# Norming of the heads before attention: query bias on TensorE, a square and a copy a tile, guard and scale in one step, three products on GpSimd

## The chip, the cores and the metric

One NeuronCore of one Trainium2 chip runs the whole program. Its engines are TensorE (PE; its weight loads are listed as PEld), VectorE (DVE), ScalarE (ACT), GpSimd (POOL) and SyncE (SP), which issues the transfers. Each engine works through its own list of instructions in the written order, and semaphores tie the lists together. The metric is the device time of one execution in microseconds; less is better.

## The reference, cut to what matters

Four sequences of 512 tokens with 256 channels pass through a bidirectional state-space block with a gated MLP and then through an attention block. The change lies in the attention block, between its layer norm and its scores:

```python
x1 = _ln(x) * (scale1 + 1.0) + shift1
qkv_bias = jnp.concatenate([q_bias, jnp.zeros_like(q_bias), v_bias])
qkv = (x1 @ mat_qkv_w.T + qkv_bias).reshape(B, L, 3, H, hd)
q, k, v = [jnp.transpose(qkv[:, :, i], (0, 2, 1, 3)) for i in range(3)]
sm = jnp.exp(jnp.minimum(scale_mul, MAX_SCALE_MUL))
q = _l2norm(q) * sm          # x / max(sqrt(sum(x * x)), 1e-12), H = 16 heads of hd = 16
k = _l2norm(k)
scores = jnp.einsum('bhqd,bhkd->bhqk', q, k)
```

So each of 16 query heads and 16 key heads of a token is divided by its length, and the query heads are scaled by a factor of their own. Only queries and values have a bias. All data are in fp32.

## The kernel before, in words

The program goes through the four sequences one after another (`batch(b)`). In each it scans 128 rows of the state-space block (the greater part of the time), then comes the residual, the MLP, the attention and the feed-forward part. The order on each engine is written out by hand; nothing is scheduled by a planner. Tokens are worked in `TT` = 4 tiles of 128. PSUM has 8 banks of 128x512 fp32, named `bank0` to `bank7`; all of them are handed from one use to the next by semaphores.

The stage that changes runs like this. The residual after the MLP is added tile by tile by VectorE (`residual_ln`, L1540), which also makes the statistics and `x_norm` (L1531). TensorE turns each tile's `x_norm` (`ln_turn`, L983) into banks 6 and 7, ScalarE shifts and scales it into `h_t` (L757), and TensorE multiplies `h_t` by the query and key weights (L1286), 128x512 a tile, into banks 4 and 5 in turn. VectorE adds the query bias on the way out (L1716, the semaphore `q_ready`), ScalarE copies the key half (L898) and squares both halves in two steps (L899, L900, `sq_ready`), VectorE sums the squares by head (L1694), ScalarE takes the root (L894), and VectorE guards it (L1699), inverts it (L1701), multiplies by the scales `qk_scale` (L1703) and multiplies the heads by the result (`unit`, L1706) into `qk_pad`, where each head has 32 lanes. Meanwhile TensorE makes the values (`value_tile`): a product of one row of ones (`ident[0:1, 0:1]` spread out) with the bias row (L1296) and two with the weights (L1299). Then it turns the normed heads (`turn_heads`, L1313) into banks 6 and 7; VectorE and ScalarE copy them to `q_t` and `k_t` (L1726, L913), and the scores begin (L1348), whose least values VectorE takes (`least`, L1732). GpSimd has nothing to do from its clearing of `qk_pad` on until `qk_unit` tells that all four products are done; then it weights the projection and later weights with the gates (L718 and on).

Buffers are reused, and the profile names them by their first owner: `inflow_tok` holds `qk`, `h_t` and the MLP's product `ab`; `states` holds `qk_sq`; `b_diag` holds the sums and their inverses; `decay` holds `qk_pad`; `dt` and `dtx_tok` hold `q_t` and `k_t`; `silu_z` holds the values. An fp32 product is recorded as two matmul records, a transpose as one; the order of the program counts products and transposes once each.

Of the kernel before, what the change touches and what calls it, by code (L numbers as in the profile page):

```python
# [7 lines left out]
ALU = mybir.AluOpType  # L8
ACT = mybir.ActivationFunctionType
# [64 lines left out]
QK_BANK = 4  # L74
# [67 lines left out]
def build(nc, inp, out):  # L142
    ctx = ExitStack()
    with ctx:
# [35 lines left out]
        qk_scale = sb("qk_scale", [P, 2 * H])  # L180
# [64 lines left out]
        norm_max = norm_sq  # L245
# [44 lines left out]
        q_scale_ready = sem("q_scale_ready")  # L290
# [82 lines left out]
        q_ready = sem("q_ready")  # L373
        k_ready = sem("k_ready")
# [4 lines left out]
        norm_max_ready = sem("norm_max_ready")  # L379
        norm_inv_ready = sem("norm_inv_ready")  # L380
        qk_inv_ready = sem("qk_inv_ready")
        qk_unit = sem("qk_unit")
        qk_turned = sem("qk_turned")
# [37 lines left out]
        out_rows = out.rearrange("b (t p) d -> b p t d", p=P)  # L421

# [189 lines left out]
        def _(pool):  # L612
# [5 lines left out]
            pool.memset(qk_scale[:, H:2 * H], -1.0).then_inc(sign_ready, 1)  # L618
# [69 lines left out]
            def batch(b, last):  # L688
# [26 lines left out]

                pool.wait_ge(res_ready, (b * 2 + 1) * TT)
                pool.wait_ge(qk_unit, (b + 1) * TT)
# [25 lines left out]
        def _(act):  # L743
# [4 lines left out]

            def ln(b, i):
# [20 lines left out]
                if i == 2:  # L770
                    for t in range(TT):
                        root(t)
                        if t:
                            shift(t - 1)
                    shift(TT - 1)
                    return
                root(0)
                root(1)
                shift(0)
                shift(1)  # L780
# [73 lines left out]
            for s in range(NS):  # L854
                if s == DT_EXP_AT[0]:
                    act.wait_ge(ssm_loaded, 16 * len(SSM))
                    act.activation(a_exp[:], a_log[:], ACT.Exp).then_inc(a_exp_done, 1)
                    act.wait_ge(cap_ready, 1)
                    act.wait_ge(sign_ready, 1)
                    act.activation(qk_scale[:, 0:H], scale_cap[:], ACT.Exp).then_inc(q_scale_ready, 1)  # L860
# [4 lines left out]
            def batch(b, last):  # L865
# [26 lines left out]
                def root(t):  # L892
# [3 lines left out]
                for t in range(TT):  # L896
                    act.wait_ge(q_ready, b * TT + t + 1)
                    act.activation(qk[:, t, D:2 * D], banks[QK_BANK + t % 2][:, D:2 * D], ACT.Copy)  # L898
                    act.activation(qk_sq[:, t, D:2 * D], banks[QK_BANK + t % 2][:, D:2 * D], ACT.Square).then_inc(k_ready, 1)  # L899
                    act.activation(qk_sq[:, t, 0:D], qk[:, t, 0:D], ACT.Square).then_inc(sq_ready, 1)  # L900
                    if t:
                        root(t - 1)
                root(TT - 1)
# [45 lines left out]
        def _(pe):  # L949
# [270 lines left out]
            def batch(b, last):  # L1220
# [49 lines left out]
                for t in range(TT):  # L1270
# [7 lines left out]
                    last.then_inc(res_mm, 1)  # L1278
                ln_turn(b, 2, 1)
                for t in range(TT):  # L1280
                    ln_wait(b, 2, t)
                    pe.wait_ge(res_ready, (b * 2 + 1) * TT + t + 1)
                    if t > 1:
                        pe.wait_ge(k_ready, b * TT + t - 1)
                    for kc in range(KD):
                        last = pe.matmul(banks[QK_BANK + t % 2], h_t[:, kc, t * P:(t + 1) * P], qkv_w[:, kc, 0:2 * D],  # L1286
                                         start=(kc == 0), stop=(kc == KD - 1))
                    last.then_inc(qk_mm, 1)
                    if t == 0:
                        ln_turn(b, 2, 2)  # L1290
                        ln_turn(b, 2, 3)

                def value_tile(t):

                    to = banks[V_BANK + t // 2][:, t % 2 * D:(t % 2 + 1) * D]
                    pe.matmul(to, ident[0:1, 0:1].to_broadcast([1, P]), row_b[0:1, V_BIAS, :], start=True, stop=False,  # L1296
# [536 lines left out]
```

## Time and profile before

| what | us |
|---|---|
| median of 3 runs | 3185.71 (3183.74 to 3186.26) |
| the profiled execution | 3181.57 |
| its span, first to last instruction | 3179.80 |
| TensorE busy in the span | 3101.2 (98%) |
| VectorE busy | 2759.0 (87%) |
| ScalarE busy | 2705.0 (85%) |
| GpSimd busy | 2484.5 (78%) |

All times below are microseconds from the start of the span. A row of a timeline merges neighbouring instructions of one kind: its second number runs from the start of the first to the end of the last, and the end of a matmul is modelled, so that the start of the next row is the surer mark. "idle before" in brackets tells how long the engine had stood idle and what ended it. The stage occurs four times, with its first head turn at about 740.6, 1520.6, 2301.6 and 3063.6.

### The profile page before, as it was taken

The numbers are of one execution on the slowest core, as the hardware profiler recorded it, in microseconds if no ns is written. First come the engines' busy times: TensorE is split into PE (matmuls) and PEld (weight loads), VectorE is DVE, ScalarE is ACT, GpSimd is POOL, SyncE is SP. The second block draws the span as 40 slices with busy tenths as digits, with TensorE's granted clock in tenths as the row PEclk, the third lists the DMA queues.
The fourth block names the chain that finished last, engine by engine and source line by source line (L and its number), as shares of the span: only waits on it lengthen the run. The fifth ranks groups of instructions, "written<-read, shape, count | busy, mean of one in ns | idle before, by whom it ended". The sixth has DMA issues, their size and how long they took to land.

```text
span 3179.8 us, 59519 instructions
## 1 busy us (share of the span) xinstructions
PE 3101.2 (98%) x23304; PEld 2630.3 (83%) x23304; DVE 2759.0 (87%) x3049; ACT 2705.0 (85%) x4496; POOL 2484.5 (78%) x638
## 2 busy tenths in 40 slices
PE   7999999999999999999999999999999999999999
PEld 6998899884699889988479988998748998888955
DVE  3999999977399999997659999999666999999963
ACT  4999999965699999995579999999458999999845
POOL 2999999971299999995139999999415999999910
PEclk9999999999999999999999999999999999999999
DMA  5222222210222222221022222222102222222100
GB/s 188 77 82 67 90 69 82 74 56 29 75 67 82 80 86 67 89 86 58 1 83 70 89 82 78 79 77 88 45 14 80 81 80 85 74 70 82 57 14 8
DMA packets 195239, 225.69 MB, mean 71 GB/s; under 512 B 77448, under 2 KB 149640, under 8 KB 193680
## 3 DMA queue, kind: packets, MB, share of 16 engines
q1 hardware_dynamic: 194960, 221.89, 22.7%
q8 instruction: 185, 3.03, 0.4%
q14 instruction: 94, 0.77, 0.1%
HBM read 217.37 MB, written 4.48 MB: 70 GB/s over the span
## 4 chain that ended last, share of the span: by engine, by line
PE 78%; POOL 11%; issue 5%; DVE 3%; ACT 1%; DMA 1%; SPq 0%; DVEq 0%; ACTq 0%; POOLq 0%
PE bank L1124 21%; PE bank L1104 16%; PE bank L1004 10%; PE bank L1105 9%; POOL states L669 7%; PE bank L1348 4%; PE bank L1100 4%; POOL y_gated L669 4%; PE bank L1369 2%; PE bank L1381 2%; PE bank L1483 2%; DVE states L1630 1%; PE bank L1179 1%; PE bank L1131 1%; PE bank L1276 1%
## 5 line engine op out<-in xcount | busy, mean ns | idle before, releaser
L669 POOL TENSOR_TENSOR states<-states,c_rows 128x2048 f32<-128x2048 f32 x336 | 1532.8, 4582 | 129.1 <-DVE states L1630 126.8
L1630 DVE TENSOR_TENSOR_SCAN states<-decay,bank 128x512 f32<-128x512 f32 x1376 | 1577.1, 1200 | 16.5 <-ACT decay L849 1.2
L849 ACT ACTIVATE decay<-dt,a_log 128x512 f32<-128x512 f32 x2048 | 1305.5, 710 | 0.0
L840 ACT ACTIVATE inflow_tok<-dtx_tok,b_tok 128x512 f32<-128x512 f32 x1536 | 995.6, 713 | 81.0 <-PE bank L1105 70.4
L1104 PE MATMUL bank<-ident,inflow_tok 128*128 128x128 f32 x5280 | 903.4, 280 | 35.6 <-DVE states L1630 18.4
L1124 PE MATMUL bank<-ident,states 128*128 128x128 f32 x5504 | 825.5, 273 | 6.1 <-DVE y_gated L1636 3.0
L1630 DVE TENSOR_TENSOR_SCAN y_gated<-decay,bank 128x512 f32<-128x512 f32 x672 | 776.7, 1201 | 12.3 <-issue 2.6
L669 POOL TENSOR_TENSOR y_gated<-y_gated,c_rows 128x2048 f32<-128x2048 f32 x168 | 770.0, 4583 | 17.8 <-DVE y_gated L1630 16.1
L1104 PEld LDWEIGHTS bank<-ident,inflow_tok 128*128 128x128 f32 x5280 | 597.7, 140 | 205.7 <-issue 88.0
L1105 PE MATMUL bank<-b_diag,dtx_tok 128*128 128x128 f32 x3520 | 680.5, 275 | 0.0
L1124 PEld LDWEIGHTS bank<-ident,states 128*128 128x128 f32 x5504 | 644.6, 141 | 14.2 <-POOL states L669 7.7
L1105 PEld LDWEIGHTS bank<-b_diag,dtx_tok 128*128 128x128 f32 x3520 | 531.5, 191 | 0.0
L1124 PE MATMUL bank<-ident,y_gated 128*128 128x128 f32 x2688 | 403.5, 273 | 1.3 <-POOL y_gated L669 0.7
L1124 PEld LDWEIGHTS bank<-ident,y_gated 128*128 128x128 f32 x2688 | 315.0, 141 | 4.6 <-POOL y_gated L669 3.8
L735 POOL TENSOR_TENSOR part<-part,x_in 128x1024 f32<-128x1024 f32 x4 | 9.4, 2354 | 302.0 <-ACT part L767 302.0
L1732 DVE TENSOR_REDUCE decay<-bank 128x1 f32<-128x512 f32 x256 | 158.9, 682 | 45.3 <-PE bank L1348 45.2
L1004 PE MATMUL bank<-xs,xproj_w 128*128 128x256 f32 x640 | 185.2, 381 | 0.9 <-ACT b_tok L812 0.5
L1348 PE MATMUL bank<-dtx_tok,dt 32*128 32x512 f32 x512 | 155.4, 693 | 3.1 <-ACT dtx_tok L913 3.1
L1100 PE MATMUL bank<-ident,inflow_tok 128*128 128x128 f32 x864 | 149.1, 282 | 0.9 <-DVE states L1630 0.5
L927 ACT ACTIVATE y_gated<-bank 128x512 f32<-128x512 f32 x176 | 92.7, 601 | 59.6 <-PE bank L1369 59.1
L718 POOL TENSOR_TENSOR x_in<-proj_w,gate 128x512 f32<-128x512 f32 x4 | 5.1, 1272 | 165.9 <-DVE decay L1706 165.9
L1100 PEld LDWEIGHTS bank<-ident,inflow_tok 128*128 128x128 f32 x864 | 97.6, 140 | 33.5 <-DVE states L1630 6.4
(174 smaller groups left out, 2596.6 us busy)
## 6 DMA issues: line engine op xcount, KB each, us to landing
c_rows<-c_spill SPq DMA_DIRECT2D x256, 512.0 KB, 3.7
b_diag<-diag_ring SPq DMA_DIRECT2D x256, 128.0 KB, 2.3
xproj_w<-in_xproj_w SPq DMA_DIRECT2D x32, 320.0 KB, 3.7
in_w<-in_in_w SPq DMA_DIRECT2D x16, 512.0 KB, 4.6
out_w<-in_out_w SPq DMA_DIRECT2D x4, 1024.0 KB, 8.2
in_w<-in_fc_w SPq DMA_DIRECT2D x8, 512.0 KB, 4.1
xproj_w<-in_w SPq DMA_DIRECT2D x8, 512.0 KB, 5.2
xproj_w<-in_fc_w SPq DMA_DIRECT2D x4, 1024.0 KB, 4.8
```

Of the source, the lines that this page charges most:

```text
L669: pool.tensor_tensor(state_row, state_row, c_row.to_broadcast([P, KI, L]), ALU.mult).then_inc(weighed, PAIRS)
L840: last_tok = act.activation(inflow_tok[:, r % SLOTS, t, :], dtx_tok[:, d, t, :], ACT.Copy, scale=b_tok[:, d, t, s:s + 1])
L849: act.activation(decay[:, r % SLOTS * KI + k, :], dt[:, d, k, :], ACT.Exp, scale=a_neg[:, d, k, s:s + 1]).then_inc(decay_ready, 1)
L927: act.activation(probs_t[v % len(probs_t)], banks[t_bank(v)], ACT.Exp, scale=-1.0).then_inc(probs_t_ready, 1)
L1004: out = pe.matmul(to[:, c], lhs, rhs[:, c], start=start and half == 0, stop=stop, skip_group_check=True)
L1100: last = pe.transpose(to[:, t * P:(t + 1) * P], tile[:, k * P:(k + 1) * P], ident[:])
L1104: pe.transpose(to[:, t * P:(t + 1) * P], inflow_tok[:, r % SLOTS, t, k * P:(k + 1) * P], ident[:])
L1105: pe.matmul(to[:, (TT - 1) * P:TT * P], dtx_tok[:, d, TT - 1, k * P:(k + 1) * P], b_diag[:, r % DIAGS, :], start=True, stop=True).then_inc ...
L1124: last = pe.matmul(banks[KI + t][:, k * P:(k + 1) * P], state_slots[r % STATES][:, k, t * P:(t + 1) * P], ident[:], is_transpose=True, sta ...
L1348: pe.matmul(score_bank(u), q_t[a, g, t * P:(t + 1) * P], k_t[a, g, :], start=True, stop=True).then_inc(scores_mm, 1)
L1630: dve.tensor_tensor_scan(state_slots[r % STATES][:, k, time], decay[:, slot, time], banks[k % INFLOW_BANKS][:, time], 0.0, ALU.mult, ALU.a ...
L1732: dve.tensor_reduce(qk_pad[:, t, g, lane:lane + 1], score_bank(u), AX.X, ALU.min).then_inc(neg_ready, 1)
```

## The change

The query bias is no longer added by VectorE: TensorE puts it into the bank with a one-row product (`query_bias`) ahead of the query and key products, which then add to it. The four tiles get banks 4, 5, 0 and 1, one each, and no longer wait for `k_ready`; and the turns of tiles 1 to 3 stand at other places. ScalarE squares a whole tile of 512 columns from the bank in one step and copies it in another; the first square stands among the shifts of `ln`. VectorE guards the root and multiplies by the inverse scale in one step (`inv_scale`, made at the start by an exponential of the negated exponent), then inverts. The products of tiles 0 to 2 are made by GpSimd from ScalarE's copy, that of tile 3 by VectorE straight from the bank, so tile 3 needs no copy.

```diff
-QK_BANK = 4
+QK_BANKS = (4, 5, 0, 1)
...
+                for t in range(TT - 1):
+                    pool.wait_ge(qk_copied, b * (TT - 1) + t + 1)
+                    pool.wait_ge(norm_inv_ready, b * TT + t + 1)
+                    pool.tensor_tensor(heads(qk_pad[:, t, :, :].rearrange("p g c -> p (g c)"), LANE)[:, :, 0:HD],
+                                       heads(qk[:, t, :], HD), norm_inv[:, t, :].unsqueeze(2).to_broadcast([P, 2 * H, HD]),
+                                       ALU.mult).then_inc(qk_unit, 1)
+
                 pool.wait_ge(res_ready, (b * 2 + 1) * TT)
-                pool.wait_ge(qk_unit, (b + 1) * TT)
                 pool.tensor_tensor(proj_g, proj_w[:], gate[:, GAMMA1, :].unsqueeze(1).to_broadcast([P, KD, D]),
                                    ALU.mult).then_inc(proj_gated, 1)
...
+            def square(b, t):
+
+                act.wait_ge(qk_mm, b * TT + t + 1)
+                act.activation(qk_sq[:, t, :], banks[QK_BANKS[t]], ACT.Square).then_inc(sq_ready, 1)
+
...
-                if i == 2:
-                    for t in range(TT):
-                        root(t)
-                        if t:
-                            shift(t - 1)
-                    shift(TT - 1)
-                    return
+                if i == 2:
+                    root(2)
+                    shift(1)
+                    root(3)
+                    shift(2)
+                    square(b, 0)
+                    shift(3)
+                    return
...
-                    act.activation(qk_scale[:, 0:H], scale_cap[:], ACT.Exp).then_inc(q_scale_ready, 1)
+                    act.activation(inv_scale[:, 0:H], scale_cap[:], ACT.Exp, scale=-1.0).then_inc(inv_scale_ready, 1)
...
-                def root(t):
+                def head_root(t):
-                for t in range(TT):
-                    act.wait_ge(q_ready, b * TT + t + 1)
-                    act.activation(qk[:, t, D:2 * D], banks[QK_BANK + t % 2][:, D:2 * D], ACT.Copy)
-                    act.activation(qk_sq[:, t, D:2 * D], banks[QK_BANK + t % 2][:, D:2 * D], ACT.Square).then_inc(k_ready, 1)
-                    act.activation(qk_sq[:, t, 0:D], qk[:, t, 0:D], ACT.Square).then_inc(sq_ready, 1)
-                    if t:
-                        root(t - 1)
-                root(TT - 1)
+                def copy_heads(t):
+                    act.activation(qk[:, t, :], banks[QK_BANKS[t]], ACT.Copy).then_inc(qk_copied, 1)
+                copy_heads(0)
+                square(b, 1)
+                head_root(0)
+                copy_heads(1)
+                square(b, 2)
+                head_root(1)
+                square(b, 3)
+                copy_heads(2)
+                head_root(2)
+                head_root(3)
...
+                def query_bias(t):
+                    pe.wait_ge(res_ready, (b * 2 + 1) * TT + t - 1)
+                    pe.matmul(banks[QK_BANKS[t]][:, 0:D], ident[0:1, 0:1].to_broadcast([1, P]), row_b[0:1, Q_BIAS, :], start=True,
+                              stop=False, skip_group_check=True)
+                def heads_tile(t):
+                    ln_wait(b, 2, t)
+                    for kc in range(KD):
+                        last = pe.matmul(banks[QK_BANKS[t]], h_t[:, kc, t * P:(t + 1) * P], qkv_w[:, kc, 0:2 * D],
+                                         start=False, stop=(kc == KD - 1), skip_group_check=True)
+                    last.then_inc(qk_mm, 1)
+                query_bias(0)
+                query_bias(1)
-                for t in range(TT):
-                    ln_wait(b, 2, t)
-                    pe.wait_ge(res_ready, (b * 2 + 1) * TT + t + 1)
-                    if t > 1:
-                        pe.wait_ge(k_ready, b * TT + t - 1)
-                    for kc in range(KD):
-                        last = pe.matmul(banks[QK_BANK + t % 2], h_t[:, kc, t * P:(t + 1) * P], qkv_w[:, kc, 0:2 * D],
-                                         start=(kc == 0), stop=(kc == KD - 1))
-                    last.then_inc(qk_mm, 1)
-                    if t == 0:
-                        ln_turn(b, 2, 2)
-                        ln_turn(b, 2, 3)
+                query_bias(2)
+                heads_tile(0)
+                ln_turn(b, 2, 2)
+                query_bias(3)
+                heads_tile(1)
+                ln_turn(b, 2, 3)
+                heads_tile(2)
+                heads_tile(3)
+                    pe.wait_ge(res_ready, (b * 2 + 1) * TT + V_BANK + t // 2 + 1)
...
-                            pe.wait_ge(qk_unit, b * TT + t + 1)
+                            if t < TT - 1:
+                                pe.wait_ge(qk_unit, b * (TT - 1) + t + 1)
+                            else:
+                                pe.wait_ge(qk_unit_last, b + 1)
...
-                def unit(t):
+                def invert(t):
-                    dve.tensor_scalar(norm_max[:, t, :], norm[:, t, :], EPS_NORM, None, ALU.max).then_inc(norm_max_ready, 1)
-                    dve.wait_ge(norm_max_ready, b * TT + t + 1)
-                    dve.reciprocal(norm_inv[:, t, :], norm_max[:, t, :]).then_inc(norm_inv_ready, 1)
-                    dve.wait_ge(norm_inv_ready, b * TT + t + 1)
-                    dve.tensor_tensor(norm_inv[:, t, :], norm_inv[:, t, :], qk_scale[:], ALU.mult).then_inc(qk_inv_ready, 1)
-                    dve.wait_ge(qk_inv_ready, b * TT + t + 1)
-                    pad = qk_pad[:, t, :, :].rearrange("p g (h e) -> p (g h) e", e=LANE)
-                    dve.tensor_tensor(pad[:, :, 0:HD], qk[:, t, :].rearrange("p (h e) -> p h e", e=HD),
-                                      norm_inv[:, t, :].unsqueeze(2).to_broadcast([P, 2 * H, HD]),
-                                      ALU.mult).then_inc(qk_unit, 1)
+                    dve.scalar_tensor_tensor(norm_over[:, t, :], norm[:, t, :], EPS_NORM, inv_scale[:], ALU.max,
+                                             ALU.mult).then_inc(norm_over_ready, 1)
+                    dve.wait_ge(norm_over_ready, b * TT + t + 1)
+                    dve.reciprocal(norm_inv[:, t, :], norm_over[:, t, :]).then_inc(norm_inv_ready, 1)
-                    dve.wait_ge(q_scale_ready, 1)
+                    dve.wait_ge(inv_scale_ready, 1)
-                for t in range(TT):
-                    dve.wait_ge(qk_mm, b * TT + t + 1)
-                    dve.tensor_tensor(qk[:, t, 0:D], banks[QK_BANK + t % 2][:, 0:D], row_b[:, Q_BIAS, :],
-                                      ALU.add).then_inc(q_ready, 1)
-                    if t:
-                        sum_squares(t - 1)
-                    if t > 1:
-                        unit(t - 2)
-                sum_squares(TT - 1)
-                unit(TT - 2)
-                unit(TT - 1)
+                sum_squares(0)
+                sum_squares(1)
+                invert(0)
+                sum_squares(2)
+                invert(1)
+                sum_squares(3)
+                invert(2)
+                invert(3)
+                dve.wait_ge(norm_inv_ready, (b + 1) * TT)
+                dve.tensor_tensor(heads(qk_pad[:, TT - 1, :, :].rearrange("p g c -> p (g c)"), LANE)[:, :, 0:HD],
+                                  heads(banks[QK_BANKS[TT - 1]], HD), norm_inv[:, TT - 1, :].unsqueeze(2).to_broadcast([P, 2 * H, HD]),
+                                  ALU.mult).then_inc(qk_unit_last, 1)
```

On TensorE, from the product with `w3` (into bank 3) to the first value tile, there stood before:

```order
L1276 MATMUL bank3<-w3,inflow_tok 128x256 x4
L983 MATMUL bank7<-ident,x_norm 128x128 [waits ln_norm]
L1286 MATMUL bank4<-qkv_w,inflow_tok 128x512 [waits res_ready,ln_ready]
L983 MATMUL bank6<-ident,x_norm 128x128 [waits ln_ready,ln_norm]
...
L983 MATMUL bank7<-ident,x_norm 128x128 [waits ln_ready,ln_norm]
...
L1286 MATMUL bank5<-qkv_w,inflow_tok 128x512 [waits res_ready,ln_ready]
...
L1286 MATMUL bank5<-qkv_w,inflow_tok 128x512 [waits k_ready,res_ready,ln_ready]
...
L1296 MATMUL bank2<-row_b,ident 128x256
```

In the changed kernel (L1296 is there the product with `w3`, L1302 the query bias, L1003 the turn, L1309 the heads' product, L1329 the value bias) the same stretch of TensorE reads:

```order
L1296 MATMUL bank3<-w3,inflow_tok 128x256 x4
L1302 MATMUL bank4<-row_b,ident 128x256 [waits res_ready]
L1302 MATMUL bank5<-row_b,ident 128x256 [waits res_ready]
L1003 MATMUL bank7<-ident,x_norm 128x128 [waits ln_norm]
...
L1302 MATMUL bank0<-row_b,ident 128x256 [waits res_ready]
L1309 MATMUL bank4<-qkv_w,inflow_tok 128x512 [waits ln_ready]
...
L1003 MATMUL bank6<-ident,x_norm 128x128 [waits ln_ready,ln_norm]
...
L1302 MATMUL bank1<-row_b,ident 128x256 [waits res_ready]
L1309 MATMUL bank5<-qkv_w,inflow_tok 128x512 [waits ln_ready]
...
L1003 MATMUL bank7<-ident,x_norm 128x128 [waits ln_ready,ln_norm]
...
L1329 MATMUL bank2<-row_b,ident 128x256 [waits res_ready]
```

Four one-row products are new. The turn of tile 1 now stands behind two of them, and the turn of tile 3 has moved from ahead of the heads of tile 1 to behind them.

On VectorE the norming of the last tile, from its sum of squares (tile 2's steps behind it are left out) to the first copy of the turned heads, was this before:

```order
L1694 TENSOR_REDUCE b_diag<-states 128x32 [waits sq_ready]
...
L1699 TENSOR_SCALAR b_diag<-b_diag 128x32 [waits norm_ready]
L1701 RECIPROCAL b_diag<-b_diag 128x32 [waits norm_max_ready]
L1703 TENSOR_TENSOR b_diag<-b_diag,qk_scale 128x32 [waits norm_inv_ready]
L1706 TENSOR_TENSOR decay<-inflow_tok,b_diag 128x32x16 [waits qk_inv_ready]
L1726 COPY dt<-bank6 128x512 [waits qk_turned]
```

The changed kernel has at the same place of VectorE's list:

```order
L1730 TENSOR_REDUCE b_diag<-states 128x32 [waits sq_ready]
...
L1735 SCALAR_TENSOR_TENSOR b_diag<-b_diag,inv_scale 128x32 [waits norm_ready]
L1738 RECIPROCAL b_diag<-b_diag 128x32 [waits norm_over_ready]
L1753 TENSOR_TENSOR decay<-bank1,b_diag 128x32x16 [waits norm_inv_ready]
L1757 COPY dt<-bank6 128x512 [waits qk_turned]
```

Two steps of three remain between root and product, and one product of four; the other three stand on GpSimd's list between the clearing of `silu_z` and the weighting of the projection:

```order
L717 MEMSET silu_z 128x2048
L722 TENSOR_TENSOR decay<-inflow_tok,b_diag 128x32x16 [waits norm_inv_ready,qk_copied] x3
L727 TENSOR_TENSOR x_in<-proj_w,gate 128x512 [waits res_ready]
L729 TENSOR_TENSOR x_in<-row_b,gate 128x256
L730 TENSOR_TENSOR x_in<-row_b,gate 128x256
```

GpSimd no longer waits for `qk_unit` ahead of the weighting; it does the three products itself, each after a tile's inverse and copy.

## Rows read from the trace of the kernel before

**Rows 1.** The page's chain that ended last, by engine.

```profile
PE 78%; POOL 11%; issue 5%; DVE 3%; ACT 1%; DMA 1%; SPq 0%; DVEq 0%; ACTq 0%; POOLq 0%
```

**Rows 2.** Chain in order of time, first batch: start us, us, what.

```profile
727.84 0.50 DVE x_norm L1531
...
728.38 0.44 PE bank L983 x2
...
740.76 0.89 PE bank L1313 x8
...
741.67 0.61 ACT dtx_tok L913
```

**Rows 3.** Timeline of TensorE, first batch: start us, us, instructions, idle before.

```profile
723.70 1.89 PE L1276 MATMUL bank<-w,inflow_tok 128*128 128x256 f32 x8
725.43 0.38 PE L983 MATMUL bank<-ident,x_norm 128*128 128x128 f32 x2
725.64 1.88 PE L1286 MATMUL bank<-qkv_w,inflow_tok 128*128 128x512 f32 x4
727.36 0.38 PE L983 MATMUL bank<-ident,x_norm 128*128 128x128 f32 x2
728.38 0.44 PE L983 MATMUL bank<-ident,x_norm 128*128 128x128 f32 x2 [0.63 <-DVE x_norm L1531]
728.65 5.37 PE L1286 MATMUL bank<-qkv_w,inflow_tok 128*128 128x512 f32 x12
733.95 0.69 PE L1296 MATMUL bank<-row_b,ident 1*128 1x256 f32 x2
734.58 1.13 PE L1299 MATMUL bank<-qkv_w,inflow_tok 128*128 128x256 f32 x4
735.64 0.69 PE L1296 MATMUL bank<-row_b,ident 1*128 1x256 f32 x2
...
740.60 1.04 PE L1313 MATMUL bank<-ident,decay 128*128 128x128 f32 x8
```

**Rows 4.** Timeline, all engines, first batch.

```profile
739.90 0.69 DVE L1706 TENSOR_TENSOR decay<-inflow_tok,b_diag 128x512 f32<-128x512 f32 x1
...
740.38 1.01 PEld L1313 LDWEIGHTS bank<-ident,decay 128*128 128x128 f32 x8
```

**Rows 5.** Timeline of TensorE, second batch.

```profile
1508.42 0.44 PE L983 MATMUL bank<-ident,x_norm 128*128 128x128 f32 x2 [0.63 <-DVE x_norm L1531]
...
1520.64 1.04 PE L1313 MATMUL bank<-ident,decay 128*128 128x128 f32 x8
```

**Rows 6.** Groups of instructions: xcount | busy us, mean ns | idle before.

```profile
L913 ACT ACTIVATE dtx_tok<-bank 128x512 f32<-128x512 f32 x16 | 9.5, 593 | 1.1 <-PE bank L1313 1.1
L1694 DVE TENSOR_REDUCE b_diag<-states 128x32 f32<-128x512 f32 x16 | 10.8, 676 | 0.0
L894 ACT ACTIVATE b_diag<-b_diag 128x32 f32<-128x32 f32 x16 | 3.7, 229 | 6.1 <-DVE b_diag L1694 6.1
L1701 DVE RECIPROCAL b_diag<-b_diag 128x32 f32<-128x32 f32 x16 | 5.6, 353 | 0.5
L1706 DVE TENSOR_TENSOR decay<-inflow_tok,b_diag 128x512 f32<-128x512 f32 x16 | 11.1, 691 | 0.5
L718 POOL TENSOR_TENSOR x_in<-proj_w,gate 128x512 f32<-128x512 f32 x4 | 5.1, 1272 | 165.9 <-DVE decay L1706 165.9
```

**Rows 7.** Windows: us, PE, PEld, DVE, ACT, POOL busy, clock, DMA.

```profile
754.00:758.00 4.00, 4.00 (x15) 1.89 (x16) 4.00 (x8) 0.83 (x2) 0.62 (x1) 0.69 0.02 4
1534.00:1538.00 4.00, 4.00 (x15) 1.86 (x12) 4.00 (x8) 0.05 (x1) 0.68 (x1) 0.50 0.00 0
```

**Rows 8.** Timeline, scores of first and second batch.

```profile
756.00 1.11 PE L1355 MATMUL bank<-ident,decay 128*128 128x128 f32 x4
...
1536.80 1.11 PE L1355 MATMUL bank<-ident,decay 128*128 128x128 f32 x4
```

**Rows 9.** Line L1680: duration ns min/median/max, first and last start.

```profile
L1680 DVE TENSOR_TENSOR states<-states,c_rows x8: 678/1594/3253, 686.6 to 3012.6; 128x512 f32<-128x512 f32 x8
```

More of the change, by code:

```diff
@@ L179, in build @@
         scale_cap = sb("scale_cap", [P, H])
-        qk_scale = sb("qk_scale", [P, 2 * H])
+        inv_scale = sb("inv_scale", [P, 2 * H])
         proj_w = sb("proj_w", [P, KD, D])
@@ L244, in build @@
         norm = norm_sq
-        norm_max = norm_sq
+        norm_over = norm_sq
         norm_inv = b_diag[:, HALF + 1, :].rearrange("p (t h) -> p t h", t=TT)
@@ L289, in build @@
         cap_ready = sem("cap_ready")
-        q_scale_ready = sem("q_scale_ready")
+        inv_scale_ready = sem("inv_scale_ready")
         mod_mm = sem("mod_mm")
@@ L372, in build @@
         v_mm = sem("v_mm")
-        q_ready = sem("q_ready")
-        k_ready = sem("k_ready")
+        qk_copied = sem("qk_copied")
         v_ready = sem("v_ready")
@@ L378, in build @@
         norm_ready = sem("norm_ready")
-        norm_max_ready = sem("norm_max_ready")
+        norm_over_ready = sem("norm_over_ready")
         norm_inv_ready = sem("norm_inv_ready")
-        qk_inv_ready = sem("qk_inv_ready")
         qk_unit = sem("qk_unit")
+        qk_unit_last = sem("qk_unit_last")
         qk_turned = sem("qk_turned")
@@ L421, in build, with heads @@
         out_rows = out.rearrange("b (t p) d -> b p t d", p=P)
+        def heads(row, e):
+            return row.rearrange("p (h e) -> p h e", e=e)
         def lead_last(bank):
@@ L617, in _ @@
             pool.memset(ring_zeros, 0.0).then_inc(zeros_ready, 1)
-            pool.memset(qk_scale[:, H:2 * H], -1.0).then_inc(sign_ready, 1)
+            pool.memset(inv_scale[:, H:2 * H], -1.0).then_inc(sign_ready, 1)
             pool.memset(minus_half[:], -0.5).then_inc(half_ready, 1)
```

## The prediction

> **What bounds the kernel now.** I read the page's chain first: TensorE carries 78% of the path that ended last and VectorE 3% [rows 1]. That average covers several stages, so I followed the chain in time through the one that changes, the norming of the heads in the first batch [rows 2]. The reader is to see who holds the path there. Until 728.33 it is VectorE with the last `x_norm`; from 728.38 to 741.65 it is TensorE alone: a turn (L983), the query and key products of three tiles (L1286), the four value tiles (L1296 and L1299), the turn of the normed heads (L1313). Only then does ScalarE take over with `dtx_tok`, the copy of the turned keys. VectorE's adds, sums and products do not appear.
>
> Then the timeline of TensorE [rows 3]. Its rows follow one another without a gap except once: the turn of tile 2 starts at 727.36 and that of tile 3 at 728.38, 1.02 us later, where a turn and its neighbour are otherwise 0.21 us apart (725.43 to 725.64). So 0.81 us are spent waiting for `x_norm`, and nothing else is. VectorE is close behind, however: its last product runs from 739.90 to 740.59, while the weights of the first turn are loaded at 740.38 and the turn starts at 740.60 [rows 3, 4]. Tile 3 is the fourth of those transposes, so the product is out before it is needed, by a few tenths. The second batch has the same gap of 0.63 us ahead of the turn and 12.22 us from it to the first head turn (1508.42 to 1520.64), as the first has (728.38 to 740.60) [rows 3, 5]. Thus two chains end almost together, and a gain on VectorE's alone is worth nothing until TensorE's becomes shorter.
>
> **The change part by part.** *TensorE gets four bias products a batch.* An operation of this shape stands in the trace: the value bias L1296, one row by 256 columns. A value tile, from one bias to the next, takes 735.64 - 733.95 = 1.69 us for six records of 256 columns. Eight such records without a bias, in tile 3 of the product with `w3`, take 725.43 - 723.70 = 1.73 us, 0.216 us each [rows 3]. Six would take 1.30, so 0.39 us of each value tile is lost around its bias. A bias that stands alone between full products therefore costs 2 x 0.216 + 0.39 = 0.82 us; the pair of tiles 0 and 1, which stand together, 4 x 0.216 + 0.39 = 1.25. Both ends: nothing lost (0.43 each, 1.73 for four) or the loss paid by each of the four (3.28). I take 0.82 twice and 1.25 once, 2.89 us, since the row is of the same operands and sizes. The Trainium skill says, in TensorEngine Tiling (Array Packing), section Key Properties, that changing the tiling mode drains TensorE. By that rule each run of one-row products pays at entry and exit, which agrees with the 0.39 us; without it the four would cost only their columns. The rule speaks against this change.
>
> *TensorE loses its wait.* The turn of tile 3 now stands behind the products of tile 1, long after its `x_norm`, so the 0.81 us go. Written out from the old rows, in the first batch: the product with `w3` ends at 725.43, the pair of biases at 726.68, turn 1 at 726.89, the bias of tile 2 at 727.71, the heads of tile 0 (1.72 us, 725.64 to 727.36) at 729.43, turn 2 at 729.64, the bias of tile 3 at 730.46, heads 1 at 732.18, turn 3 at 732.39, heads 2 at 734.11, heads 3 at 735.83. The old values and turn took 740.60 - 733.95 = 6.65 after 0.14 us of change-over, so the first head turn starts at about 742.62 in place of 740.60: 2.02 us later in a batch. The waits that the bias products carry (`res_ready` of the attention's input) are for residuals of tiles finished before them; the value tiles' waits likewise. `k_ready` is no longer waited for, but the rows show no gap in the twelve products, so this gives nothing. Each heads tile needs its `h_t`; ScalarE makes it under 1 us after a turn, in the same order as before, and every turn now precedes its heads by over a microsecond.
>
> *The norming chain gets shorter, under cover of TensorE.* VectorE loses four adds, four guards and three products, gains none. ScalarE's copy of 512 columns out of a bank costs 593 ns by L913, and I take the same for a square of 512; a sum of squares 676, a root 229, a reciprocal 353, the one-step guard and scale about what a small two-input step takes, estimated at 0.2; the last product 691 [rows 6]. After heads 2 (734.11, landed 0.2 later) there remain at most two squares, one copy, three roots, two sums, three guards with reciprocals and the product: 1.78 + 0.69 + 1.35 + 1.66 + 0.69 = 6.2 us if nothing overlapped, so 740.5 at the latest. GpSimd's products have the size of L718, 1272 ns. The first reciprocal follows turn 3 (732.39) by a shift, a copy, a square and a root on ScalarE and a guard on VectorE, at an estimated 736.2, and three products end at 740.0 if not held up. All of this lies before 742.62; the cover is 2.1 us, and a delay beyond it would be paid in full.
>
> *Behind the turn* nothing is rearranged. GpSimd's gated weights start after its last product, near where they started (740.74). ScalarE's value and key copies and VectorE's first copy follow TensorE as they did, and the scores after them, so the 2.02 us move the rest of the batch whole. Four batches: 8.1 us. The profiled execution took 3181.57 us, 1.77 more than its span, and lies 4.1 below the median of the runs, 3185.71, and under the fastest of them. The same step on its time gives 3189.7, on the median 3193.8.
>
> *The clock.* In the scores that follow, the granted clock falls to its lower level: 0.69 as a mean over 754 to 758 in the first batch, 0.50 (1.2 GHz) over 1534 to 1538 in the second [rows 7]. TensorE was just then running the 32-row score products, waiting for VectorE between them. The turn L1355 then starts 15.40 us after the first head turn in the first batch (740.60 to 756.00), 16.16 in the second (1520.64 to 1536.80) [rows 3, 5, 8]. A shifted stage can meet that fall earlier or later: 0.76 us a batch, from -2.3 us (three batches become like the first) to +0.8.
>
> **The rivals.** *The bias products hide (3182.5).* If each cost under 0.2 us, the 0.81 us removed would outweigh them; were they free, the turns would start 0.81 us earlier, VectorE's chain being then out in time, and the result is 3185.7 - 3.2 = 3182.5, no change that can be measured. It would need gaps in TensorE's rows, and there is one of 0.81 us, while two records cannot stream in less than 0.43. For it: only that record ends are modelled. Chance 0.09.
>
> *Only the columns count (3189.1).* If the 0.39 us belong to the value tiles and not to a bias, the three losses go: 2.02 - 1.17 = 0.85 a batch, 3.4 in all. Against it: L1296 starts and L1299 starts are 0.63 apart, again and again. Chance 0.14.
>
> *VectorE and GpSimd get in each other's way (3203).* L1680, a VectorE step with two operands in SBUF, took 678 to 3253 ns for 512 columns, beside GpSimd's last weighing; L1706 with the same shape and GpSimd idle took 691 [rows 6, 9]. In the changed kernel each guard step reads two SBUF tiles while GpSimd multiplies the tile before. If each of the guards of tiles 1 to 3 waited out a product, the products would start at 736.2, 738.1 and 739.9, and VectorE's own would end at about 742.5: just hidden. It decides from there: if reciprocals or sums waited too, two more products, 2.5 us, would reach the path, 745.0, and the total is 4.4 us a batch, 3185.7 + 17.6 = 3203. The Trainium skill, GPSIMD Engine Reference, section Key points, names this contention for two-SBUF-input steps; the range of L1680 agrees, and by that rule alone the guards would wait and the products not. Chance 0.08.
>
> **How the numbers follow.** The forecast has 0.69. Its own range is 3191.5 to 3196.2: from the clock's -2.3 to the loss paid by all four biases (+1.6) with the clock's +0.8. For 8 in 10 I reach down past the columns-only case, 3187.5, and up to 3198. A measurement of this kernel can tell about 0.2%, 6.4 us, from no change: slower means over 3192.1. The forecast lies above that unless clock and spread (the runs before range over 2.5 us) take 1.7 us from it; I give it 0.62 of its 0.69. With the collision, slower 0.70; the other part and the two rivals that end lower make 0.30, of which 0.04 goes to faster, for biases that hide and a clock that falls kindly in all batches, and 0.26 to the same.
>
> **What would show it.** Right: bias rows on TensorE 0.63 us ahead of what follows, no idle before the turn of tile 3, the path through the stage TensorE throughout, the first head turn some 2.0 us later after the end of the product with `w3` (17.2 us against 15.2), VectorE's last product over early. Wrong: head turns that wait for GpSimd or VectorE; bias products at 0.43 us; or a start of the turns before 17 us.

## The result

The changed kernel takes 3191.86 us (median of 9 runs, 3187.87 to 3198.38), the kernel before 3183.28 in the same comparison (9 runs, 3181.40 to 3186.26): ratio 1.0028, interval 1.0019 to 1.0037, so some 6 to 12 us slower. The profiled execution took 3191.34 us, with a span of 3189.6, 9.8 more than before.

In the chain that ended last, TensorE has gained four points [rows 1]:

```profile
PE 82%; POOL 8%; issue 4%; DVE 3%; ACT 2%; DMA 1%; SPq 0%; DVEq 0%; ACTq 0%; POOLq 0%
```

The timeline of TensorE in the first batch, as [rows 3] before (L1296 is the product with `w3`, L1302 the query bias, L1003 a turn, L1309 the heads, L1329 and L1332 the values, L1349 the head turns):

```profile
723.09 1.89 PE L1296 MATMUL bank<-w,inflow_tok 128*128 128x256 f32 x8
724.91 1.13 PE L1302 MATMUL bank<-row_b,ident 1*128 1x256 f32 x4
725.97 0.44 PE L1003 MATMUL bank<-ident,x_norm 128*128 128x128 f32 x2
726.34 0.69 PE L1302 MATMUL bank<-row_b,ident 1*128 1x256 f32 x2
726.96 1.98 PE L1309 MATMUL bank<-qkv_w,inflow_tok 128*128 128x512 f32 x4
728.78 0.38 PE L1003 MATMUL bank<-ident,x_norm 128*128 128x128 f32 x2
729.09 0.69 PE L1302 MATMUL bank<-row_b,ident 1*128 1x256 f32 x2
729.72 1.98 PE L1309 MATMUL bank<-qkv_w,inflow_tok 128*128 128x512 f32 x4
731.54 0.38 PE L1003 MATMUL bank<-ident,x_norm 128*128 128x128 f32 x2
731.75 3.60 PE L1309 MATMUL bank<-qkv_w,inflow_tok 128*128 128x512 f32 x8
735.28 0.69 PE L1329 MATMUL bank<-row_b,ident 1*128 1x256 f32 x2
...
741.93 1.04 PE L1349 MATMUL bank<-ident,decay 128*128 128x128 f32 x8
```

No row carries an idle time any more. From the start of the last tile of the product with `w3` to the first head turn it is 741.93 - 723.09 = 18.84 us, where it was 740.60 - 723.70 = 16.90 [rows 3]: 1.94 us more. The four batches have 1.94, 1.95, 1.93 and 1.94, 7.8 us together. Each bias that stands alone starts 0.62 or 0.63 us ahead of its heads (726.34 to 726.96), the pair 1.06 ahead of the turn.

The timelines of VectorE and GpSimd in the same stretch show the norming (L1735 is the guard with the scale, L1738 the reciprocal, L722 GpSimd's product, L1753 VectorE's):

```profile
735.09 1.06 POOL L722 TENSOR_TENSOR decay<-inflow_tok,b_diag 128x512 f32<-128x512 f32 x1 [36.48 <-DVE b_diag L1738]
...
735.46 0.73 DVE L1735 SCALAR_TENSOR_TENSOR b_diag<-b_diag,inv_scale 128x32 f32<-128x32 f32 x1
...
736.72 1.06 POOL L722 TENSOR_TENSOR decay<-inflow_tok,b_diag 128x512 f32<-128x512 f32 x1 [0.58 <-DVE b_diag L1738]
...
737.04 0.79 DVE L1735 SCALAR_TENSOR_TENSOR b_diag<-b_diag,inv_scale 128x32 f32<-128x32 f32 x1
...
738.13 0.13 DVE L1735 SCALAR_TENSOR_TENSOR b_diag<-b_diag,inv_scale 128x32 f32<-128x32 f32 x1
...
738.65 1.06 POOL L722 TENSOR_TENSOR decay<-inflow_tok,b_diag 128x512 f32<-128x512 f32 x1 [0.87 <-DVE b_diag L1738]
738.68 0.69 DVE L1753 TENSOR_TENSOR decay<-bank,b_diag 128x512 f32<-128x512 f32 x1
```

All four products are out by 739.71, 2.2 us ahead of the turns. Two of the guards take 0.73 and 0.79 us where one without a neighbour takes 0.13, and they end when GpSimd's product does (735.46 + 0.73 = 736.19, against 735.09 + 1.06 = 736.15).

### The profile page after: what moved, and what is told of

The parts are those of the page before. It is cut to its first block, busy times and chain, and to the rows that moved or that the text cites. A ratio compares the mean times of both kernels' runs of the same rounds, so it can differ in the third digit from the quotient of the medians.

```text
span 3189.6 us, 59523 instructions
## 1 busy us (share of the span) xinstructions
PE 3111.6 (98%) x23336; PEld 2637.1 (83%) x23336; DVE 2745.7 (86%) x3005; ACT 2704.2 (85%) x4476; POOL 2496.2 (78%) x650
## 4 chain that ended last, share of the span: by engine, by line
PE 82%; POOL 8%; issue 4%; DVE 3%; ACT 2%; DMA 1%; SPq 0%; DVEq 0%; ACTq 0%; POOLq 0%
PE bank L1144 23%; PE bank L1124 17%; PE bank L1024 10%; PE bank L1125 10%; POOL states L672 5%; PE bank L1120 4%; PE bank L1384 4%; POOL y_gated L672 2%; PE bank L1405 2%; PE bank L1417 2%; PE bank L1519 2%; DVE states L1666 2%; PE bank L1199 1%; PE bank L1309 1%; PE bank L1151 1%
## 5 line engine op out<-in xcount | busy, mean ns | idle before, releaser
L1124 PEld LDWEIGHTS bank<-ident,inflow_tok 128*128 128x128 f32 x5280 | 597.5, 141 | 210.8 <-issue 93.4
L722 POOL TENSOR_TENSOR decay<-inflow_tok,b_diag 128x512 f32<-128x512 f32 x12 | 12.7, 1057 | 150.7 <-DVE b_diag L1738 150.7
L1405 PE MATMUL bank<-dt,dtx_tok 32*128 32x512 f32 x512 | 125.0, 630 | 0.0
```

Source lines behind the costliest of these rows:

```text
L1124: pe.transpose(to[:, t * P:(t + 1) * P], inflow_tok[:, r % SLOTS, t, k * P:(k + 1) * P], ident[:])
L1405: pe.matmul(banks[t_bank(v)], k_t[a, g, kt * P:(kt + 1) * P], q_t[a, g, :], start=True, stop=True).then_inc(scores_t_mm, 1)
```

## The experiments

Three rivals to the forecast's account were to be settled: only the columns cost; GpSimd and VectorE hold each other up; part of the loss lies elsewhere. The table sums up what the timelines gave, per batch, from the start of the product with `w3` to the first head turn ("the stage" below) and to the first score product. These are its marks in TensorE's timeline of the first batch, before and after, which with the head turns at 740.60 and 741.93 give the first two rows:

```profile
718.16 5.34 PE L1276 MATMUL bank<-w,inflow_tok 128*128 128x256 f32 x24
742.41 1.13 PE L1348 MATMUL bank<-dtx_tok,dt 32*128 32x512 f32 x4 [0.78 <-ACT dtx_tok L913]
```

```profile
717.55 5.34 PE L1296 MATMUL bank<-w,inflow_tok 128*128 128x256 f32 x24
743.74 1.13 PE L1384 MATMUL bank<-dtx_tok,dt 32*128 32x512 f32 x4 [0.78 <-ACT dtx_tok L933]
```

The ratios are to the kernel before as it ran beside each; its medians there were 3183.18 to 3184.10. A ratio whose interval holds 1 shows no change.

| kernel | head turn, us | first score, us | median, us | ratio (interval) |
|---|---|---|---|---|
| before | 22.44 | 24.25 | 3183.28 | 1 |
| after | 24.38 | 26.19 | 3191.86 | 1.0028 (1.0019 to 1.0037) |
| no query bias | 21.54 | 23.36 | 3179.51 | 0.9988 (0.9980 to 0.9997) |
| query bias, 128 rows | 23.26 | 25.08 | 3189.14 | 1.0018 (1.0009 to 1.0027) |
| both biases, 128 rows | 21.71 | 23.52 | 3180.02 | 0.9990 (0.9981 to 0.9999) |
| before, turn moved | 23.31 | 25.13 | 3186.89 | 1.0012 (1.0003 to 1.0021) |
| and own banks | 21.54 | 23.70 | 3180.72 | 0.9993 (0.9984 to 1.0002) |
| and values, 128 rows | 19.98 | 23.70 | 3192.84 | 1.0028 (1.0019 to 1.0038) |
| and TensorE kept busy | 19.98 | 23.71 | 3181.17 | 0.9994 (0.9985 to 1.0003) |
| after, products twice | 24.38 | 26.20 | 3195.55 | 1.0040 (1.0027 to 1.0053) |
| both 128 rows, value behind | 20.41 | 22.92 | 3180.99 | 0.9991 (0.9982 to 0.9999) |

**No query bias.** The four products are left out, and with them the query bias. The wait that they carried and the opening of the bank pass to the heads' product (not shown).

```diff
...
-                query_bias(0)
-                query_bias(1)
                 ln_turn(b, 2, 1)
-                query_bias(2)
                 heads_tile(0)
                 ln_turn(b, 2, 2)
-                query_bias(3)
                 heads_tile(1)
...
```

> The changed kernel with its four query-bias products left out (so the query bias is not added at all); everything else of the change stays. Theory (the four one-row products on TensorE are the whole loss, the rest lies under TensorE's cover): from the start of the product with w3 to the first head turn 24.38 - 2.75 = 21.6 us, 0.8 us a batch less than before the change, no idle on TensorE ahead of the turns; about 3.2 us faster than before, ratio 0.999. Rival (part of the loss comes from GpSimd's products, the guards or the squares): the stage stays above 22.4 us, with head turns that wait for GpSimd or VectorE, and the time is not below that of before.

In the first batch the product with `w3` and the head turns start here:

```profile
716.57 5.34 PE L1296 MATMUL bank<-w,inflow_tok 128*128 128x256 f32 x24
...
738.11 1.04 PE L1346 MATMUL bank<-ident,decay 128*128 128x128 f32 x8
```

That is 21.54 us, as in every batch, 2.84 less than with the products and 0.90 less than before; the rest of the change is then a small gain, 0.9988. The whole loss is the four products.

**Query bias by 128 rows.** The bias tile holds the same row in all 128 partitions, so the identity times it is the bias on every token.

```diff
-                    pe.matmul(banks[QK_BANKS[t]][:, 0:D], ident[0:1, 0:1].to_broadcast([1, P]), row_b[0:1, Q_BIAS, :], start=True,
+                    pe.matmul(banks[QK_BANKS[t]][:, 0:D], ident[:], row_b[:, Q_BIAS, :], start=True,
                               stop=False, skip_group_check=True)
```

> The changed kernel, but the query bias is put in by the identity and all 128 (equal) rows of the bias tile, so that these products have the same 128 rows as their neighbours. Theory (0.39 us are lost around each run of one-row products, three runs a batch): the stage becomes 24.38 - 1.17 = 23.2 us, ratio to before 1.0012, about 4.7 us below the changed kernel. Rival (only the columns cost, the loss belongs to something else): the stage stays at 24.4 us and the ratio at 1.0028.

23.26 us: 1.12 of the expected 1.17 come back, with the same columns streamed. The timeline of TensorE now has 0.44 from a bias to its heads where 0.62 stood; the columns-only rival falls. The ratio, 1.0018, has the expected 1.0012 within its interval.

```profile
724.11 1.89 PE L1296 MATMUL bank<-w,inflow_tok 128*128 128x256 f32 x8
...
726.70 0.38 PE L1003 MATMUL bank<-ident,x_norm 128*128 128x128 f32 x2
726.92 0.60 PE L1302 MATMUL bank<-row_b,ident 128*128 128x256 f32 x2
727.36 1.88 PE L1309 MATMUL bank<-qkv_w,inflow_tok 128*128 128x512 f32 x4
729.07 0.38 PE L1003 MATMUL bank<-ident,x_norm 128*128 128x128 f32 x2
```

The loss goes with the change between one row and 128, not with each product: up to turn 1, behind the pair of biases, 0.29 us come back (2.88 to 2.59), up to turn 2, behind a single one, 0.44 (2.81 to 2.37), and up to turn 3 another 0.39. The weight loads show what changed. These are the loads for the bias of tile 2 and for the heads of tile 0, in the changed kernel and, below, in this run:

```profile
726.33 0.29 PEld L1302 LDWEIGHTS bank<-row_b,ident 1*128 1x128 f32 x2 [0.17 <-issue]
726.96 0.30 PEld L1309 LDWEIGHTS bank<-qkv_w,inflow_tok 128*128 128x128 f32 x2 [0.33 <-ACT inflow_tok L771]
```

```profile
726.81 0.30 PEld L1302 LDWEIGHTS bank<-row_b,ident 128*128 128x128 f32 x2
727.14 0.41 PEld L1309 LDWEIGHTS bank<-qkv_w,inflow_tok 128*128 128x128 f32 x2
```

By 128 rows the heads' weights are loaded from 727.14 on, 0.22 us ahead of their product (727.36) and while the bias still runs; behind one row the load starts at 726.96, with the product. The loads of the bias take no longer by one row (0.29 against 0.30), so the spread-out element as weights, which this edit removes too, is not what costs. Why a change of rows keeps the load back, no run shows.

**Both biases by 128 rows.** The same edit in `value_tile` as well.

> As the run before, and the four value biases as well by the identity and 128 rows. Theory (the loss of 0.39 us is at every one-row product between full ones): another 4 x 0.39 = 1.56 us a batch, the stage 21.65 us, 0.8 us a batch less than before the change; ratio 0.999. Rival (only the columns cost): 24.4 us and 1.0028. If VectorE's or GpSimd's chain becomes the later one, TensorE shows an idle time ahead of the head turns and the stage ends between 21.65 and 22.4.

21.71 us, another 1.55 for the expected 1.56. Two value biases in TensorE's timeline of the first batch:

```profile
737.84 0.59 PE L1329 MATMUL bank<-row_b,ident 128*128 128x256 f32 x2
739.14 0.59 PE L1329 MATMUL bank<-row_b,ident 128*128 128x256 f32 x2
```

A value tile takes 739.14 - 737.84 = 1.30 us, the six records' worth that the prediction worked out; it was 1.69 [rows 3]. This version keeps the change and is faster than both kernels; than the one before by 0.1%, with an interval that ends just under 1 (0.9981 to 0.9999).

**The kernel before with the turn moved.**

```diff
-                    if t == 0:
-                        ln_turn(b, 2, 2)
-                        ln_turn(b, 2, 3)
+                    if t < 2:
+                        ln_turn(b, 2, t + 2)
```

> The kernel before with one edit: the turn of tile 3 stands behind the heads of tile 1, as in the changed kernel. Theory (TensorE is the path, the wait ahead of that turn costs 0.81 us, and VectorE's chain moves up with the earlier heads): the stage goes from 22.44 to 21.6 us, 3.2 us in all, ratio 0.999. Rival (VectorE's chain of adds, sums and products is the bound as soon as TensorE is earlier): the head turns wait for its last product, the stage stays between 22.0 and 22.4 us, ratio 1.000.

Neither: 23.31 us, 0.87 more than before. The chain in order of time shows why (L757 is ScalarE's shift of tile 3, L898 and L899 its copy and square of tile 0):

```profile
728.18 0.80 ACT inflow_tok L757 x2
728.98 0.27 ACT inflow_tok L898
729.26 0.28 ACT states L899
729.54 0.14 issue
729.67 3.67 PE bank L1286 x8
```

TensorE's timeline has the wait:

```profile
729.67 3.67 PE L1286 MATMUL bank<-qkv_w,inflow_tok 128*128 128x512 f32 x8 [1.53 <-ACT states L899]
```

The heads of tile 2 go into tile 0's bank and wait for `k_ready`, and ScalarE comes to tile 0 only behind the shift that the moved turn allows. Whether the moved turn pays with a bank for each tile is the next run's question.

**And own banks.** As the run before, with `QK_BANKS = (4, 5, 0, 1)` and without the wait for `k_ready`.

> The kernel before with two edits: the turn of tile 3 behind the heads of tile 1, and banks 4, 5, 0 and 1, one for each tile, so that no heads product waits for ScalarE's squares of an earlier tile. Theory (the 1.5 us that the moved turn cost by itself were the wait for the shared bank, k_ready): TensorE's own work needs 21.6 us from the product with w3 to the head turns, where 22.44 stood, and VectorE's chain, some 10 us from its first sum to its last product, now ends last, at an estimated 22.0: head turns at 21.6 to 22.0, ratio 0.9990 to 0.9995. Rival (the wait was not for the bank): the stage stays at 23.3 and the ratio at 1.0012.

TensorE is ready at 21.54 us, 1.77 earlier than with two banks and 0.90 earlier than before; the wait was for the bank. Its row of head turns is then stretched by VectorE, as the chain in order of time shows (L1703 is the norming's product, L1310 a turn):

```profile
739.76 0.70 DVE decay L1703
740.46 0.04 issue
740.50 0.78 PE bank L1310 x5
```

Tile 3's product ends at 740.46, 22.1 us after the start at 718.35, and the last five turns stand behind it. The first score comes at 23.70, 0.55 ahead of before; the ratio, 0.9993, is as forecast, but its interval holds 1.

**And value biases by 128 rows.**

> As the run before, with the value biases by the identity and 128 rows. Theory (two chains end together, and VectorE's longer norming bounds the stage once TensorE's is shorter): TensorE would be ready at 20.1 us but the last head turn of the first four waits for VectorE's product; the stage and the time are those of the run before to 0.3 us a batch. Rival (TensorE alone sets the stage): 20.1 us, 9 us faster than before, ratio 0.997.

The stage is as the theory had it: TensorE ready at 19.98, first score at 23.70 as in the run before. But the time is 9 us longer than before, and 12 longer than in the run before, which no theory here expected. The timeline of TensorE and the windows (us, busy of PE, PEld, DVE, ACT, POOL, granted clock, DMA) of the first batch:

```profile
738.05 0.38 PE L1310 MATMUL bank<-ident,decay 128*128 128x128 f32 x2
738.80 0.33 PE L1310 MATMUL bank<-ident,decay 128*128 128x128 f32 x1 [0.36 <-DVE decay L1703]
740.23 0.76 PE L1310 MATMUL bank<-ident,decay 128*128 128x128 f32 x5 [1.10 <-DVE decay L1703]
741.77 2.07 PE L1345 MATMUL bank<-dtx_tok,dt 32*128 32x512 f32 x4 [0.78 <-ACT dtx_tok L913]
```

```profile
741.00:743.00 2.00, 1.23 (x4) 0.53 (x4) 0.28 (x1) 0.60 (x1) 2.00 (x4) 0.57 0.02 4
743.00:749.00 6.00, 6.00 (x22) 3.39 (x21) 2.51 (x5) 1.36 (x3) 6.00 (x2) 0.50 0.00 0
```

TensorE stands idle for 0.36, 1.10 and 0.78 us, and between 741 and 743 the granted clock falls to its lower level, 1.2 GHz (0.57 as the mean of this window, 0.50 from 743 on): the first four score records take 2.07 us where they took 1.13. The first batch went so, and the fourth; there the first turn of the greatest values came 42.7 and 41.2 us after the start, in the two others, with the same waits, 38.1 and 37.7. What decides between them is not shown.

**And TensorE kept busy.** Four identity products without use fill the two waits for VectorE.

```diff
+                            if not g and not i:
+                                for _ in range((0, 0, 1, 3)[t]):
+                                    pe.matmul(banks[TURN_BANK + 1][:, 0:D], ident[:], qkv_w[:, 0, 0:D], start=True, stop=True)
                             pe.wait_ge(qk_unit, b * TT + t + 1)
```

> The run with own banks and value biases by 128 rows (ratio 1.0028, though its first scores came as early as in the run with own banks alone, 23.7 us after the start of the product with w3), plus four identity products of 256 columns (0.43 us each, result unused) that TensorE makes while it waits for VectorE: one ahead of the third head turn, three ahead of the fourth. Theory (the wait itself costs nothing more than with own banks alone; the loss came from the granted clock, which fell to its lower level right behind that wait in two of four batches and made the first scores twice as slow): with TensorE occupied the clock stays at its upper level until the scores, the first turn of the greatest values comes 37.2 to 38.1 us after the start in every batch, ratio 0.999 to 1.000. Rival (the loss has another cause, such as the order of the copies): the fillers change nothing or add up to 0.2 us a batch, ratio 1.003.

The first score at 23.71 as before, the clock at 1.00 in the windows where it had been 0.57 and 0.50, the greatest values' turn at 37.1 to 38.1 in all four batches, ratio 0.9994; so the clock was the loss:

```profile
741.00:743.00 2.00, 1.23 (x6) 0.50 (x7) 0.39 (x2) 0.60 (x1) 2.00 (x4) 1.00 0.01 4
743.00:749.00 6.00, 6.00 (x45) 3.52 (x45) 4.96 (x8) 3.26 (x6) 6.00 (x2) 1.00 0.00 0
```

This is also the fair measure for the rest of the change. With the value biases by 128 rows in both, the old norming and the bias on VectorE, given own banks and a busy TensorE, have the first score at 23.71; the new norming, shared with GpSimd, with the query bias on TensorE by 128 rows, has it at 23.52. That is 0.19 us a batch, and the ratios, 0.9994 and 0.9990, cannot be told apart.

**Products twice.** Each of GpSimd's three products is made twice in the changed kernel, with a wait for the first between.

> The changed kernel with each of GpSimd's three products made twice, with a wait for the first between. Theory (GpSimd's products and the guards that wait beside them end 2.2 us ahead of the head turns that read them, and this cover is all that hides them): 3 x 1.06 = 3.2 us more and a tenth for each wait, so 1.0 to 1.5 us a batch come to the path, the head turn of tile 2 waits for GpSimd, ratio 1.004 to 1.005. Rival (GpSimd's work is far from the path): no change, ratio 1.0028. Other rival (guards wait out each product in full and pass it on): 3 us or more a batch, ratio above 1.006.

A miss in size: the head turns stay at 24.38 and the first score at 26.20, so nothing reaches the path. Timelines of the first batch:

```profile
735.51 1.06 POOL L723 TENSOR_TENSOR decay<-inflow_tok,b_diag 128x512 f32<-128x512 f32 x1 [36.49 <-DVE b_diag L1743]
...
740.95 1.06 POOL L727 TENSOR_TENSOR decay<-inflow_tok,b_diag 128x512 f32<-128x512 f32 x1
...
742.35 1.04 PE L1354 MATMUL bank<-ident,decay 128*128 128x128 f32 x8
```

The sixth product ends at 742.01, 0.34 ahead of the turns. I had added 3.2 us to the old end, but the products had stood 0.6 and 0.9 us apart, waiting for inverses, and the extra ones filled these gaps. The ratio, 1.0040 from four runs, lies in the forecast range, but not for its reason: the stage does not show it, and the interval overlaps with that of 1.0028.

**A value tile behind the head turns.** From the version with both biases by 128 rows, `value_tile(TT - 1)` moves behind `turn_heads(0)`, and ScalarE copies its bank after the first keys.

> The changed kernel with both biases by 128 rows, and the last value tile moved behind the first head turns, where TensorE stands idle for 0.78 us until ScalarE has copied the keys; ScalarE copies these values after the first keys. Theory (TensorE is the path up to the head turns, and its idle time behind them hides that tile): the head turns start 0.86 us earlier, at 20.9 us, unless GpSimd's last product, at 21.05 in the run with both biases by 128 rows, makes tile 2 wait 0.1 to 0.2; 3 us below that run, ratio 0.998. Rival (the tile's 0.86 us are paid behind the turn, or the copies hold up the first scores): the first least value is taken no earlier than there, ratio 0.999.

The turns start at 20.41 us and the first score at 22.92 in three batches (23.21 in the first), 0.6 us less than with the tile ahead (0.3 in the first). GpSimd now reaches the path: in TensorE's timeline of the first batch the turn of tile 2 waits for its third product,

```profile
738.76 0.87 PE L1353 MATMUL bank<-ident,decay 128*128 128x128 f32 x6 [0.31 <-POOL decay L722]
```

and in the others it starts some 0.2 us behind its place. The first turn is earlier than I had written because the tile's bias goes with it: 1.30 us, not 0.86. The time, 0.9991, is not to be told from that version's 0.9990, and the forecast 0.998 lies outside its interval (0.9982 to 0.9999): the 2.1 us of the four stages are within the noise.

## Why the prediction was right

*What bounds the stage.* That TensorE's and VectorE's chains ended almost together before held: with TensorE's 0.90 us shorter (own banks) VectorE's product is waited for, and the first score gains 0.55. That only TensorE's length counts in the changed kernel held too: without the query bias, or with one or both biases by 128 rows, the head turns start when TensorE's own work is done, and the first score follows 1.81 or 1.82 us later, as before.

*The four products.* 2.89 us were forecast, the run without them gives 2.84. The split was right too: 1.12 us are change-over (forecast 1.17), and the rest, 1.72, is eight records of 0.215. The Trainium skill's rule, in TensorEngine Tiling (Array Packing), section Key Properties, that a change of tiling mode drains the engine, agrees with this: from a bias to its heads the same columns took 0.44 us by 128 rows in place of 0.62. That one row against 128 is a change of mode in that rule's sense is inferred; the trace shows only that the next weights are not loaded ahead there.

*The wait ahead of tile 3's turn.* 0.81 us were forecast, 0.90 came (22.44 to 21.54). One sentence of this step was too simple: that the end of `k_ready` "gives nothing" holds for the old order alone. In the kernel before, with the turn moved and two banks, the wait for it is 1.53 us and the stage 0.87 longer; with a bank for each tile it is 0.90 shorter. The gain thus comes from the moved turn and the own banks together; the turn alone loses there.

*The norming under cover.* It held, with two errors of size that did not matter: GpSimd's product takes 1.06 us, not 1.27, and two guards of four took 0.5 and 0.6 us more than the 0.2 allowed. The collision of VectorE with GpSimd, a rival, thus happens, but a guard waits for one product and neither reciprocals nor sums wait, the case that the rival had worked out as just hidden. The Trainium skill, GPSIMD Engine Reference, section Key points, names the contention; the 0.73 and 0.79 us agree with it.

*The sum.* 2.02 us a batch were forecast and 1.94 measured, 8.1 and 7.8 us in all; the medians lie 8.6 apart. By the mark that the prediction named, the end of the product with `w3`, the turns start 17.02 us later (741.93 - 724.91), for a forecast of 17.2 and a sign of being wrong under 17; the change-over to the first bias lengthens that product's last tile from 1.73 to 1.82 us, so its start is the better mark. The level was less sure than the step: the forecast stood on a median of 3185.71 for the kernel before, which took 3183.28 beside the changed one, so that 3191.86 lies at the lower end of the forecast's own range and just under the 3192.1 that was to mean slower. That the kernel is slower is shown by the ratio.

The span's 9.8 holds 2.0 more than the stage's 7.8. Up to the start of the last feed-forward product, counted from the product with `w3`, the four batches are 7.4 longer together; the fall of the clock in the scores, met at another place, gives 0.4 back, within the -2.3 to +0.8 allowed. The other 2.4 lie outside, in the scans, which the change doesn't touch. Over the traces of the eleven kernels each such stretch varies by 2 to 5 us; where these 2.4 come from was not tested.

## What to carry to other kernels

An operation moved to the engine that holds the path costs its full length there, however small it is, while what it frees on the others is worth only the cover that they lacked: read from the timeline which of two nearly equal chains has no gaps before taking work from the other. Put a row bias into PSUM with as many rows as the neighbouring products have, here the identity and a bias tile spread over all partitions; it cost 0.43 us against 0.82 (the 0.43 of two records of 256 columns and the 0.39 by which a value tile's 1.69 fell to 1.30). And moving a step may need a buffer of its own to be worth anything: the turn alone made the stage longer, with a bank a tile it made it shorter.

## What was not expected of the hardware

A short wait of TensorE can cost a multiple of its length by the clock: with 0.36, 1.10 and 0.78 us idle ahead of the scores, the granted clock fell from 2.4 to 1.2 GHz in two of four batches, and the scores' first part was 5.5 and 3.2 us longer there than with four useless products of 0.43 us each in the first two waits, which kept the clock up in all four batches at no cost.

Between these products, where the number of rows stayed the same, TensorE's next weights were loaded 0.22 us ahead, beside the running product; between one row and 128 they were loaded only when their own product began, and each run of one-row products between full ones lost about 0.4 us.

A guard of 32 columns with both operands in SBUF took 0.73 to 0.79 us beside a GpSimd product that had just begun and 0.13 to 0.18 without one; in every batch it ended 0.05 us after that product, which itself kept its 1.06 us. Beside such a product a sum (0.69), VectorE's product with one operand in a bank (0.69) and, in the run with products made twice, a reciprocal (0.35) were not held up.
